# Right sides for attention, made while X and Y run: twelve in X instead of fourteen, two in Y, and five reordered transfers and cuts

## The reference

```python
def _rmsnorm(x, w):
    var = jnp.mean(jnp.square(x), axis=-1, keepdims=True)
    return x * jax.lax.rsqrt(var + EPS) * w
memory_proj = jnp.einsum('bme,de->bmd', memory, W_mem)
scores = jnp.einsum('bnd,bmd->bnm', hidden_states, memory_proj) / jnp.sqrt(jnp.float32(D))
attn = jax.nn.softmax(scores, axis=-1)
memory_context = jnp.einsum('bnm,bmd->bnd', attn, memory_proj)
gate_input = jnp.concatenate([hidden_states, memory_context], axis=-1)
gate = jax.nn.sigmoid(jnp.einsum('bnf,df->bnd', gate_input, W_gate) + b_gate)
fused = hidden_states + gate * memory_context
return _rmsnorm(fused, norm_w)
```

## Time and profile before

| | |
|---|---|
| median of 3 runs | 953.23 us (952.24 to 953.51) |
| the profiled execution | 952.82 us, span 951.0 us |
| TensorE busy | 925.2 us (97%) |
| VectorE busy | 741.5 us (78%) |
| ScalarE busy | 420.0 us (44%) |
| mean granted TensorE clock | 0.991 |
| moved by DMA | 191.70 MB, 202 GB/s in the mean |

### The profile page before, as it was taken

How to read it: one execution, slowest core, us unless ns; L and a number is a source line. 1 busy time by engine, 2 the same in 40 slices (tenths; PEclk the granted TensorE clock), 3 DMA queues, 4 the chain that set the end, 5 groups by cost and what they waited for, 6 DMA issues and landing times.

```text
span 951.0 us, 13163 instructions
## 1 busy us (share of the span) xinstructions
PE 925.2 (97%) x5084; PEld 807.4 (85%) x5084; DVE 741.5 (78%) x1013; ACT 420.0 (44%) x652; POOL 53.9 (6%) x74
## 2 busy tenths in 40 slices
PE   9999999999999979999999969999999999999996
PEld 8878888888888859999999958888888888888884
DVE  5986667767666859777777648889888888888887
ACT  5442223223222215444445445555555555555553
POOL 0000000000000000000000001111111111111002
PEclk9999999999999999999999989999999999999999
DMA  9425655665467664556667945555555454555542
GB/s 350 180 113 188 224 183 177 241 227 195 160 226 247 230 243 156 178 181 231 219 238 263 388 165 200 185 192 197 175 175 176 184 176 175 173 187 200 199 177 89
DMA packets 46958, 191.70 MB, mean 202 GB/s; under 512 B 4784, under 2 KB 6832, under 8 KB 37808
## 3 DMA queue, kind: packets, MB, share of 16 engines
q1 hardware_dynamic: 46608, 190.34, 55.8%
q10 hardware_dynamic: 288, 0.52, 0.2%
HBM read 132.12 MB, written 58.72 MB: 201 GB/s over the span
## 4 chain that ended last, share of the span: by engine, by line
PE 86%; DMA 5%; DVE 5%; issue 1%; ACT 1%; SPq 1%; POOL 0%; DVEq 0%; POOLq 0%; ACTq 0%
PE psum L1198 29%; PE psum L1200 28%; PE psum L1199 28%; DMA c_raw<-in_c 2%; DVE g_l L728 1%; DMA g_raw<-in_g 1%; DMA xa_raw<-in_xt 1%; PE psum L1280 1%; DMA xs_raw<-in_xt 1%; DMA wb_low_spill<-wp_l 0%; DVE z L839 0%; DVE xs_l L728 0%; DVE xsum_l L728 0%; DVE wn_l L728 0%; ACT xh L484 0%
## 5 line engine op out<-in xcount | busy, mean ns | idle before, releaser
L1198 PE MATMUL psum<-g1h,xh 128*128 128x512 f32 x448 | 175.6, 392 | 7.8 <-DVE z L839 7.6
L1199 PE MATMUL psum<-g_l,xh 128*128 128x512 f32 x448 | 175.3, 391 | 0.0
L1198 PEld LDWEIGHTS psum<-g1h,xh 128*128 128x128 f32 x448 | 84.7, 189 | 26.7 <-issue 9.3
L1200 PE MATMUL psum<-g1h,xs_l 128*128 128x512 f32 x256 | 100.4, 392 | 0.0
L1199 PEld LDWEIGHTS psum<-g_l,xh 128*128 128x128 f32 x448 | 84.7, 189 | 17.5
L484 ACT ACTIVATE xh<-xs_raw 128x512 fp32r<-128x512 f32 x64 | 40.3, 632 | 127.3 <-PE psum L1200 127.3
L1101 DVE TENSOR_TENSOR zb<-psum,zb 128x512 f32<-128x512 f32 x112 | 76.6, 684 | 16.5 <-PE psum L1200 16.4
L1200 PE MATMUL psum<-g1h,xsum_l 128*128 128x512 f32 x192 | 74.7, 389 | 0.0
L1198 PE MATMUL psum<-yh,ws_h 128*128 128x256 f32 x256 | 72.6, 284 | 0.2
L1200 PE MATMUL psum<-yh,ws_l 128*128 128x256 f32 x256 | 72.4, 283 | 0.0
L839 DVE TENSOR_TENSOR z<-psum,bias 128x512 f32<-128x512 f32 x64 | 44.1, 689 | 33.4 <-PE psum L1200 33.4
(11 more groups left out here) (172 smaller groups left out, 2572.7 us busy)
## 6 DMA issues: line engine op xcount, KB each, us to landing
xs_raw<-in_xt SPq DMA_DIRECT2D x16, 1024.0 KB, 6.7
z_spill<-z SPq DMA_DIRECT2D x16, 1024.0 KB, 8.5
zb<-z_spill SPq DMA_DIRECT2D x16, 1024.0 KB, 7.0
xrow<-in_x SPq DMA_DIRECT2D x30, 512.0 KB, 6.5
out<-xrow SPq DMA_DIRECT2D x30, 512.0 KB, 3.8
xb_raw<-in_xt SPq DMA_DIRECT2D x8, 1024.0 KB, 8.5
xa_raw<-in_xt SPq DMA_DIRECT2D x8, 1024.0 KB, 4.9
y_spill<-y SPq DMA_DIRECT2D x16, 512.0 KB, 9.5
```

The source lines that it names most:

```text
L1198: nc.tensor.matmul(tile, ah, mh, start=start, stop=False, skip_group_check=True)
L1199: nc.tensor.matmul(tile, ah, ml, start=False, stop=False, skip_group_check=True)
L1200: return nc.tensor.matmul(tile, al, mh, start=False, stop=stop, skip_group_check=True)
```

## The change

- Block 0 of either m is no longer made in X. `WP` has six entries, N_WP is 12. In Y's pair 0, SP loads both raw blocks (`wb0_raw`, where the low parts will be); in pair 2 ScalarE and VectorE cut them in place. They are neither stored nor read back.
- The high parts of block 0 and the tiles `ct_h`, `ct_raw` change places in SBUF; in the last pair, `yt`'s and `ct`'s low cuts move on VectorE from the first product to the second and third.
- In a batch of X, SP loads x first, then stores the block before.
- `xb` and a quarter of `wq` are loaded after the last block's stores, in batch 12.
- `c` of batch 1 is loaded ahead of Y's last stores; `zb[1]` goes ahead of `norm`; ScalarE cuts this `c` after `mem_copy(0,2)`.
- In the first batch of X, G1's low part for T4 is cut one product later, and the sums of x for batch 1 are spread over three products.

```diff
-        HIGH_AT = [A21_AT, A21_AT + 4, 113, 117, 129, 133] + [33 + 4 * i for i in range(8)]
+        HIGH_AT = [157, 109, 113, 117, 129, 133] + [33 + 4 * i for i in range(8)]
+        wb0_raw = [at(f"wb{m}_raw", [PART, 2, BANK], F32, LOW_AT[m]) for m in range(2)]
-        ct_h = at("ct_h", [PART, KE, M], F32R, 157)
-        ct_raw, ct_l = raw_low("ct", [PART, KE, M], 109)
+        ct_h = at("ct_h", [PART, KE, M], F32R, A21_AT)
+        ct_raw, ct_l = raw_low("ct", [PART, KE, M], A21_AT + 4)
...
-        WP = [0, 1, B22, T1, T3, T2, T4]
+        WP = [1, B22, T1, T3, T2, T4]
@@ SP, batches of X
             for b in range(B):
-                if 1 <= b <= N_WP:
-                    store_wp(b - 1)
-                if b == N_WP:
-
-                    sp.wait_ge(wp_stored, 2 * DMA * N_WP)
-                    sp.dma_start(xb_raw[0][:, :, :], xt[1]).then_inc(xb_in[0], DMA)
-                    load_wq(0)
                 if b < B - 1:
                     sp.wait_ge(gx_mm, P7 * (b + 1))
                 if b + 2 < B:
                     sp.dma_start(xs_raw[b % 2][:, :, :], xt[b + 2]).then_inc(x_in[b % 2], DMA)
+                if 1 <= b <= N_WP:
+                    store_wp(b - 1)
                 if b < N_WP:
                     load_wp(b)
+                elif b == N_WP:
+
+                    sp.wait_ge(wp_stored, 2 * DMA * N_WP)
+                    sp.dma_start(xb_raw[0][:, :, :], xt[1]).then_inc(xb_in[0], DMA)
+                    load_wq(0)
                 elif b == B - 2:
@@ SP, pairs of Y
-                    for i in ((), (0,), (1,), (2,), (3,), (4,), (5, 6), ())[s]:
+                    for i in ((), (), (1,), (2,), (3,), (4,), (5, 6), ())[s]:
                         load_wb_low(i)
-
-
-            load_wb_high(0)
+                else:
+                    for m in range(2):
+                        sp.dma_start(wb0_raw[m][:, :, :], (wt, kd)[m][:, 0:2, HALF[0]]).then_inc(wb0_in[m], DMA)
+
+
             load_wb_high(1)
@@ SP, into attention
+            sp.wait_ge(t_mm, 2)
+            sp.dma_start(c_raw[:, :, :], c[1]).then_inc(c_in, DMA)
             store_y(SB - 1)
+            sp.dma_start(zb[1][:, :, :], zd[1]).then_inc(zb_in[1], DMA)
             sp.dma_start(norm[:, :], norm_w.rearrange("(a d) -> a d", a=1).to_broadcast((PART, D))
                          ).then_inc(norm_in, DMA)
-            sp.dma_start(zb[1][:, :, :], zd[1]).then_inc(zb_in[1], DMA)
-            sp.wait_ge(t_mm, 2)
-            sp.dma_start(c_raw[:, :, :], c[1]).then_inc(c_in, DMA)
@@ ScalarE
-                if P7 <= n - XH < GX_LAST - P7 and (n - XH) % P7 == 4:
+                if P7 <= n - XH < P7 * (N_WP + 1) and (n - XH) % P7 == 4:
                     wp_cut_high((n - XH) // P7 - 1)
+            def wb0_cut_high(m):
+                act.wait_ge(wb0_in[m], DMA)
+                copy(wb_h[m][0][:, :, :], wb0_raw[m][:, :, :]).then_inc(wb0_high, 1)
...
+                    if s == 2 and i in (1, 4):
+                        wb0_cut_high(i == 4)
...
                     exps(b + 1)
-                    c_cut_high(b + 1)
+                    if b >= 1:
+                        c_cut_high(b + 1)
                 else:
                     tanh_quarter(0)
                 mem_copy(b, 2)
+                if b == 0:
+                    c_cut_high(1)
@@ VectorE
                 if b == 0:
                     if i == 0:
                         g1_cut(B22)
-                    elif i == 1:
+                    elif i == 2:
                         g1_cut(T4)
-                    elif i == 3:
-                        for j in range(4):
-                            x_sums(1, j)
-                elif b + 1 < B:
-                    if i == 2:
+                if b + 1 < B:
+                    if i == (1 if b == 0 else 2):
                         x_sums(b + 1, 0)
                         x_sums(b + 1, 1)
...
+            def wb0_cut(m):
+                dve.wait_ge(wb0_high, m + 1)
+                low(wb_l[m][0][:, :, :], wb0_raw[m][:, :, :], wb_h[m][0][:, :, :]).then_inc(wb0_low, 1)
...
+                    if s == 2 and i in (2, 6):
+                        wb0_cut(i == 6)
                     if s == SB - 1:
-                        if i == 0:
+                        if i == 1:
                             yt_cut(0)
+                        elif i == 2:
                             ct_cut(0)
@@ TensorE
-                        pe.wait_ge(wbh_in[i], 2 * DMA)
-                        if i == 0:
-                            pe.wait_ge(wbl_in, 2 * P7 * DMA)
+                        if i >= 1:
+                            pe.wait_ge(wbh_in[i], 2 * DMA)
+                        else:
+                            pe.wait_ge(wb0_low, 2)
+                            pe.wait_ge(wbl_in, 2 * (P7 - 1) * DMA)
```

More of the change, by code:

```diff
@@ L177, in build @@
                                                      sem("wp_stored"))
+        wb0_in = [sem(f"wb0_{m}_in") for m in range(2)]
+        wb0_high, wb0_low = sem("wb0_high"), sem("wb0_low")
         wbh_in = [sem(f"wbh{i}_in") for i in range(P7)]
@@ L236, in w_slice @@
             return tile[:, k // 4, :, part, k % 4, :]
-        WP = [0, 1, B22, T1, T3, T2, T4]
-        WP_FROM = {0: [(0, 0)], 1: [(1, 0)], B22: [(1, 1)], T1: [(0, 1), (0, 0)], T3: [(1, 1), (0, 1)],
+        WP = [1, B22, T1, T3, T2, T4]
+        WP_FROM = {1: [(1, 0)], B22: [(1, 1)], T1: [(0, 1), (0, 0)], T3: [(1, 1), (0, 1)],
                    T2: [(1, 1), (0, 1), (0, 0)], T4: [(1, 0)]}
-        WP_SUMS = {0: 0, 1: 0, B22: 0, T1: 1, T3: 1, T2: 2, T4: 1}
+        WP_SUMS = {1: 0, B22: 0, T1: 1, T3: 1, T2: 2, T4: 1}
         wp_blocks = [(m, i) for m in range(2) for i in WP]
```

## The result

| | before | changed |
|---|---|---|
| median | 952.51 us (10 runs) | 949.68 us (10 runs) |
| range | 951.62 to 953.51 | 946.71 to 951.30 (9 of the 10) |
| profiled execution, its span | 952.82, 951.0 | 949.02, 947.2 |

Ratio 0.9967, 95% interval 0.9956 to 0.9978: the change is a gain of 0.33%, 2.8 us. I had forecast 6.8 us and 942 to 949.8: the median stands just inside the range, at its slow edge, and the gain is well under half of the forecast one. One execution of the changed kernel, at 1542 us with a granted clock of 0.557, is left out of the ratio and the range. The profiled execution gained 3.8 us.

What follows compares the result with a forecast made beforehand. TensorE was taken as the bound, other engines and transfers counting only where it stands still. Terms -8.8 - 0.4 + 0.5 + 1.0 + 0.9 = -6.8 took 952.8 to 946.0 us, range 942 to 949.8.

Steps and rivals of the forecast that it cites:

- W1: TensorE's 7.05 us wait in the last batch, behind VectorE waiting for `xa`: gone, -8.8 us (bounds -7.5 and -9.7).
- W0: TensorE's 0.51 us wait at the first batch: gone, -0.4 us (bounds -0.7 and 0).
- blocks behind x, T2: Batches of X: block stores queue behind x, delaying the third load of T2, a three-load block: +0.5 us (-0.3 to +2.5).
- `ct`'s cut ahead of scores(0): Last Y pair: VectorE's later low cut of `ct` delays scores(0) and attention's load queue: +1.0 us (0 to +1.3).
- W2: TensorE's 7.39 us wait in attention's first batch: moves one product on, from C's load to `yt`'s, 8.0 us; net +0.9.
- The rival of 936 us: Attention's first batch: W2 gone as well because `yt` lands by 550, giving 936 us; chance 0.12.
- The slow clock: Attention's first batch: slow matmuls fall on the sixth product, behind the moved stop, costing +1.5 to +2.5 us.

Runs made afterwards that it cites:

- run 1: Changed kernel with only the order in a batch of X put back, the block before stored ahead of the load of x: 944.36 us, ratio 0.9914.
- run 2: Kernel before, fourteen blocks, with only x loaded ahead of the block's stores in a batch of X: 958.52 us, ratio 1.0067.
- run 7: Changed kernel, x still first, but for block T2 VectorE's sums and cut and ScalarE's cut one product later: 945.57 us, ratio 0.9919.
- run 10: Changed kernel unaltered, measured again as a second sample of its spread and T2 stops: 949.98 us, ratio 0.9972.
- run 4: Changed kernel with `yt` and `ct` of batch 2 loaded right behind C's second load, ahead of Y's last stores: 941.15 us, ratio 0.9876.
- run 6: Changed kernel with only `yt`'s and `ct`'s low cuts both back in VectorE's first product of the last Y pair: 947.69 us, ratio 0.9953.
- run 8: Changed kernel with `xb` and the quarter of `wq` loaded in batch 14 right ahead of `xa`, instead of batch 12: 950.83 us, ratio 0.9974.
- run 3: Kernel before with only C's second load ahead of Y's stores, `zb` ahead of `norm`, ScalarE's cut behind the `mem` copy: 952.72 us, ratio 1.0006.
- run 5: Changed kernel with stores ahead of x, `yt` and `ct` loaded behind C, both low cuts back in the first product: 933.87 us, ratio 0.9799.
- run 9: Changed kernel, x still first, T2's sums and cuts one product later, `yt`/`ct` loaded early, both low cuts in the first product: 933.79 us, ratio 0.9801.

## Why the prediction was wrong

Of the five terms four came out in the profile, each within its bounds, and one did not. From the starts of matmuls in the two profiles:

| term | forecast | profile |
|---|---|---|
| W1, with its slow clock and the fourth Y product | -8.8 | -9.2 (7.21 and 2.46 gone, 0.45 more at the Y product) |
| W0, first batch | -0.4 | -0.7 |
| blocks behind x, T2 | +0.5 | **+3.4** (2.10 and 1.62, less 0.30 before) |
| `ct`'s cut ahead of scores(0) | +1.0 | +1.1 (1.41, less 0.27 before) |
| W2 moved one product on | +0.9 | +1.0 (7.46 and 2.53 of clock, less 7.55 and 1.49) |
| sum | -6.8 | -4.4; span -3.8 |

- **The step that failed** is the term for the blocks of X behind x: "I count 0 to 1.2 us later, twice", taken as +0.5. The mechanism was right (T2 at its limit, third load, sum ahead of the `z` addition; runs 1, 2 and 7 show it), the size was not: the profile has +3.4, above even my bound of +2.5. Two steps of the count were wrong. First, I had the stores landed 7.4 us after the batch's end, 4.9 for x and 1.24 for each store; they are there after 8.7 (147.44 + 7.12, for an end at 145.86). The stores did follow x by 1.3 and 1.2 us, as I had it, but x itself took 6.2 us and not 4.9. Second, I took it that the loads behind win back what the stores lose. Before, T2's stores had landed 5.6 us after the batch's end; 8.7 is 3.1 more (2.7 more at the block of m = 1), and of these the third load won back 0.4 (6.6 us to landing instead of 7.0) for m = 0 and 1.4 (6.5 instead of 7.9) for m = 1. It landed 16.3 us after the batch's end (155.52 + 6.6), where it had landed 13.5 after it (171.95 + 7.0, for an end at 165.4). For m = 0 TensorE paid 2.1 of these 2.8 us, since that block was not quite at its limit; the earlier trace rows show the other one, and that one paid its 1.3 in full. With 3.4 in place of 0.5 the sum is -3.9, and the profiled execution gained 3.8.
- **A cost that the sum has no term for** is the slow clock behind a T2 stop. I priced it for W1 and W2 only. It is absent from the changed kernel's first profile, and costs 1.6 us in that of run 10, the same kernel, and 1.65 us in that of run 4. After run 2's stop of 3.36 us the clock stayed up.
- **The same order by itself** costs 5.3 us in the medians (run 1) and 6.0 in the kernel before (run 2), more than the profile's 3.4. One profile is one draw of these landings: the pair of stops reads 3.4, 4.3, 2.4, 4.0 and 3.1 us in the profiles of the changed kernel and of runs 4, 6, 8 and 10, whose programs at T2 are the same, and the clock behind them and the stop in attention's first batch vary as well. The median's gain of 2.8 us against the profile's 3.8 lies within that spread.
- **The range.** Taken at their bounds, the five terms as I listed them come to 942.7 to 950.7 us, not to the 949.5 that I gave for the forecast's slow end. It is by luck that 949.68 falls inside the range of 942 to 949.8.
- **W1** was right in cause and size. Run 8 splits it: 5.6 us the wait for the stores, 2.2 the bytes ahead of `xa`. The landing of `xa` was not: 5.65 us after its issue instead of 4.9, the same slip as with x, covered here by the slack. VectorE's string of sums, not TensorE, set the new start of the fourth Y product, with a stop of 0.72 us there.
- **W2** was right against the plain reading of the change. C's load was the wait that the profile named, and bringing it forward gained nothing (run 3), because `yt` stood behind the same bytes. The size is less sure than the table looks: the stop reads 7.3 us in the changed kernel's first profile and 6.7 in run 10. The rival of 936 us at 0.12 did not come about; run 4 shows what it would have taken, and run 5 that such a time was to be had: `yt` needed not to wait for Y's last stores.
- **`ct`'s cut** did what I said; its price is 1 us in the profile, and 1 to 2 by run 6.
- **The slow clock.** I took 1.5 to 2.5 us for it behind the moved stop; it was 2.53, with all 12 matmuls slow after the stop of 7.3 us, where 6 or 7 were after the stop of 7.4 us before. The Trainium skill's page TensorE: Matmul & The Clock Gate, Part 1, says of a kernel's start that the same kernel shows different counts of slow matmuls from run to run, and advises against fitting one. The traces agree for stops too: behind the second T2 stop the changed kernel has no slow matmul in its first profile and eight in that of run 10.

## What to carry to other kernels

When a transfer is moved ahead of others, add up what waits for the ones that it passes, by their landing and not by their bytes: a store whose landing gates the next load costs its delay once more. A wait that ends last is worth only the distance to the wait behind it; list what the same engine asks for next, and where that stands in the same queue, before counting the gain. And where a load is already at its limit (a wait of 0.4 us that TensorE hardly feels), every microsecond more is paid in full, and the clock may add as much again; moving the instructions that wait by one product returned 4 us here, and the order of the queue was then worth nothing (run 9 against run 5).

## What was unexpected of the hardware

- With 1 MB of x issued ahead of it (1.6 us ahead, at T2), a block's second store lands 7.4 us after its issue in the median, against 4.0. x takes longer too when the stores follow soon. In the changed kernel's profile, with the first store 1.2 us behind x, it takes 6.2 and 5.7 us at the two T2 blocks; one batch later, where VectorE's cut was late and the first store left 2.7 us behind x, it takes

```profile
xs_raw<-in_xt SPq DMA_DIRECT2D x1, 1024.0 KB, 4.8
```

  I had reckoned with transfers that pass one behind the other, and had read the 4.9 us of `xb` in the earlier trace rows as the price of 1 MB in an empty queue; behind that load came other loads, not stores. Whether it is the stores as such or only their distance that tells, no run here takes apart.
- In five profiles with the same program at T2 the same two loads stop TensorE by 0.9 to 2.6 us each, and not alike from one execution to the next.
- The time of an execution of the changed kernel goes with its granted clock: 946.71 us at 0.994, 948.4 to 949.7 at 0.992, 950.4 to 951.3 at 0.990. In run 2 it is 956.1 us at 0.991 and 962.4 at 0.985. Kernels with hardly a stop left (runs 5 and 9) hold 0.997 or 0.998 and spread by some 1 us or less. A stop is paid for in its own length and, in some executions, in slow matmuls behind it.
